# Query, key and value loads in one instruction, the output bias on TensorE

## The reference, cut to what matters

```python
def _L1_attn_ref(x, Wqkv, bqkv, Wout, bout):            # the second attention
    qkv = x @ Wqkv.T + bqkv
    ...                                                   # split into q, k, v of 16 heads
    attn = softmax(einsum('hbqd,hbkd->hbqk', q, k) * scale)
    o = einsum('hbqk,hbkd->hbqd', attn, v)
    return o_joined @ Wout.T + bout

def _L2_attn_ref(x, W_attn, W_proj):                      # the third attention
    q, k, v = split(x @ W_attn, 3)
    att = polymax(masked(einsum('bhid,bhjd->bhij', q, k) / sqrt(8)))
    # polymax(s) = (s*s + 1 if s > 0 else 1 - s/100) / 1000
    return einsum('bhij,bhjd->bhid', att, v) @ W_proj
```

## Time and profile before

| | |
|---|---|
| time, median of three runs | 1426.34 us |
| the profiled execution's own time | 1429.44 us |
| its span | 1427.6 us |
| TensorE busy in the span | 1166.2 us (82%) |
| VectorE busy | 1044.9 us (73%) |
| ScalarE busy | 727.0 us (51%) |
| GpSimd busy | 423.7 us (30%) |
| mean granted TensorE clock | 0.922 |
| second attention, about | 410 to 632 us of the span |
| third attention, about | 686 to 912 us of the span |

### The profile page before, as it was taken

One profiled execution on the slowest core, in us unless ns is written; L12 is line 12 of the kernel. 1 busy time (PEld: TensorE's weight loads), 2 busy tenths in 40 slices (PEclk: granted clock), 3 DMA queues, 4 the chain that ended last, 5 costly groups with the idle time before them and its releaser, 6 DMA issues.

```text
span 1427.6 us, 27186 instructions
## 1 busy us (share of the span) xinstructions
PE 1166.2 (82%) x9362; PEld 835.4 (59%) x9362; DVE 1044.9 (73%) x2899; ACT 727.0 (51%) x1186; POOL 423.7 (30%) x639
## 2 busy tenths in 40 slices
PE   5989898999987777758677878687779888888887
PEld 3666667888863333337444444576667445557776
DVE  7888875666666777736778998778886676768886
ACT  4445433333334666646476777443434566654442
POOL 5545441000033342212545554213122233201110
PEclk9999998999995999978798999798899899999999
DMA  8000000000000000000000000000000000000001
GB/s 344 1 1 1 1 1 0 0 0 0 0 1 1 1 1 0 1 1 1 1 1 1 0 1 2 1 1 1 1 1 2 1 3 0 2 2 1 1 1 30
DMA packets 5846, 14.64 MB, mean 10 GB/s; under 512 B 240, under 2 KB 4464, under 8 KB 5360
## 3 DMA queue, kind: packets, MB, share of 16 engines
q1 hardware_dynamic: 5744, 13.33, 2.5%
HBM read 12.28 MB, written 1.05 MB: 9 GB/s over the span
## 4 chain that ended last, share of the span: by engine, by line
issue 33%; PE 30%; DVE 18%; DVEq 6%; POOLq 5%; ACT 5%; POOL 4%; ACTq 0%
PE PS L1899 5%; PE PS L1908 3%; PE PS L1290 2%; PE PS L1203 2%; PE PS L1118 2%; POOL trs L416 2%; PE PS L1095 2%; PE PS L1487 1%; DVE w_l0f L2421 1%; PE PS L1224 1%; PE PS L1117 1%; PE PS L1230 1%; DVE sbuf L2089 1%; DVE h L1961 1%; DVE mx L2182 1%
## 5 line engine op out<-in xcount | busy, mean ns | idle before, releaser
L2182 DVE TENSOR_REDUCE mx<-PS 128x2 f32<-128x512 f32 (+1 forms) x256 | 155.1, 620 | 73.7 <-PE PS L1234 32.9
L737 ACT ACTIVATE w_l0f<-PS 128x512 f32<-128x512 f32 (+1 forms) x256 | 136.8, 543 | 96.1 <-PE PS L1241 46.7
L414 POOL TENSOR_TENSOR tve<-tmv,eps 128x2 f32<-128x2 f32 x64 | 14.7, 229 | 496.4 <-DVE tmv L1970 297.2
L1899 PE MATMUL PS<-hT_padded,w_l0f 128*128 128x256 f32 x512 | 122.2, 385 | 0.0
L1899 PEld LDWEIGHTS PS<-hT_padded,w_l0f 128*128 128x128 f32 x512 | 94.7, 194 | 11.0
L1027 ACT ACTIVATE sg<-PS 128x512 f32<-128x512 f32 x64 | 38.2, 597 | 120.3 <-PE PS L1899 120.3
L1658 PE MATMUL PS<-w_l2f,y 128*128 128x128 f32 x512 | 75.8, 295 | 18.7 <-ACT y L900 9.5
L1658 PEld LDWEIGHTS PS<-w_l2f,y 128*128 128x128 f32 x512 | 71.3, 208 | 26.7 <-ACT y L900 16.3
L2421 DVE SCALAR_TENSOR_TENSOR w_l0f<-w_l0f 128x768 f32<-128x768 f32 x64 | 67.5, 1055 | 17.8 <-ACT w_l0f L812 16.5
L3083 DVE TENSOR_TENSOR y<-sg,PS 128x512 f32<-128x512 f32 x64 | 43.9, 687 | 49.9 <-ACT sg L1027 42.6
L1908 PE MATMUL PS<-w_l0f,y 128*128 128x128 f32 x512 | 69.0, 278 | 6.1 <-DVE y L3083 6.1
(11 more groups left out here) (499 smaller groups left out, 3309.5 us busy)
## 6 DMA issues: line engine op xcount, KB each, us to landing
w_l0f<-in_l0f SPq DMA_DIRECT2D x1, 3076.0 KB, 17.7
w_l2f<-in_l2f SPq DMA_DIRECT2D x1, 2214.0 KB, 18.8
w_l3f<-in_l3f SPq DMA_DIRECT2D x1, 1736.0 KB, 22.6
w_l0a<-in_l0a SPq DMA_DIRECT2D x1, 960.0 KB, 7.6
result<-X SPq DMA_DIRECT2D x1, 896.0 KB, 4.6
X<-in_x SPq DMA_DIRECT2D x1, 768.0 KB, 10.9
PT<-in_cbf SPq DMA_DIRECT2D x1, 640.0 KB, 8.7
w_l1f<-in_l1f SPq DMA_DIRECT2D x1, 582.0 KB, 14.8
```

Of the source, the lines that this page charges most:

```text
L737: act.activation(P8[:, hh % 8, 0:width], PS[:, hh % 2, 0:width], ACT.Exp, scale=SM_SCALE).then_inc(a["pt"], 1)
L1899: ins = pe.matmul(PS[:, 2 * (c % 2) + g, b * L:(b + 1) * L], w("l0f", "w1")[:, at:at + P], hT[:], start=True, stop=True)
L2182: dve.tensor_reduce(mx[:, hh, 0:nm], PS[:, 2 + hh % 2, 0:nm * keys].rearrange("p (t k) -> p t k", t=nm), AX.X, ALU.max).then_inc(a["mx"], 1)
```

## The change

Queries, keys and values of a tile get one buffer with three parts, and there are two such buffers, which tiles use in turn. The first is new in name only (qf, kf and vf in one piece); the second lies in the last 768 columns of H1, a buffer that these layers don't use until the end of the third attention. With that, a load is one instruction of 3 x 128 columns. In the second attention the output bias is put into Y by a matmul of one row (a row of ones as weights, the bias as the moving row) ahead of the output projection, which accumulates on it; the statistics and the normalisation read Y in PSUM. In the third attention the factor 1/1000 moves from the load of the values to the copy of the outputs. The conditions that a load waits for are the same.

```diff
-        qf, kf, vf = (sb("qf", [P, T * NH, HD]), sb("kf", [P, T * NH, HD]), sb("vf", [P, T * NH, HD]))
+        qkv0 = sb("qkv0", [P, 3, T * NH, HD])
+        qf, kf, vf = (qkv0[:, n] for n in range(3))
...
-        vfs = (vf[:], cb_flat[:, 4 * 384:4 * 384 + T * NH * HD].rearrange("p (n d) -> p n d", d=HD))
+        qkvs = (qkv0[:], H1[:].rearrange("p n d -> p (n d)")[:, NB * T * D - 3 * T * D:]
+                .rearrange("p (k n d) -> p k n d", k=3, d=HD))
+        vfs = tuple(b[:, 2] for b in qkvs)
...
                         for t in range(T):
-                            ins = pe.matmul(Y[:, t, :], oT[:, t * P:(t + 1) * P], w(name, "wout"), start=True, stop=True)
+                            if l == L1_ATTN:
+                                pe.matmul(Y[:, t, :], w("const", "ones")[0:1, :], w(name, "bout")[0:1, :],
+                                          start=True, stop=False)
+                            ins = pe.matmul(Y[:, t, :], oT[:, t * P:(t + 1) * P], w(name, "wout"),
+                                            start=l == L3_ATTN, stop=True)
                         ins.then_inc(y_ready, 1)
...
                     def load_qkv(u, t, par, bank=7):
                         dve.wait_ge(a["qkv"], u * LOADS[l] + (t + 1))
+                        if l == L1_ATTN:
+                            three = lambda b: b.rearrange("p (k f) -> p k f", k=3)
+                            dve.tensor_tensor(qkvs[par][:, :, t * NH:(t + 1) * NH, :].rearrange("p k n d -> p k (n d)"),
+                                              three(PS[:, bank, 0:3 * D]), three(w(name, "bqkv")), ALU.add).then_inc(a["ld"], 1)
+                            return
...
                         dve.wait_ge(y_ready, u + (res0[l] + 1))
-                        if l == L1_ATTN:
-                            dve.tensor_tensor(acc[:], Y, w(name, "bout").unsqueeze(1).to_broadcast([P, T, D]), ALU.add)
-                            dve.drain()
-                        tail_stats(result)
+                        tail_stats(Y)
...
-                        dve.tensor_copy(qf[:, at], PS[:, bank, 0:D].rearrange("p (a d) -> p a d", d=HD))
-                        dve.tensor_copy(kf[:, at], PS[:, bank, D:2 * D].rearrange("p (a d) -> p a d", d=HD))
-                        dve.tensor_scalar(vfs[par][:, at], PS[:, bank, 2 * D:3 * D].rearrange("p (a d) -> p a d", d=HD),
-                                          1e-3, None, ALU.mult).then_inc(a["ld"], 1)
+                        dve.tensor_copy(qkvs[par][:, :, t * NH:(t + 1) * NH, :].rearrange("p k n d -> p k (n d)"),
+                                        PS[:, bank, 0:3 * D].rearrange("p (k f) -> p k f", k=3)).then_inc(a["ld"], 1)
...
                         for t in range(T):
-                            ins = dve.tensor_copy(ov[:, t], O[:, t, :, :, 0:HD])
+                            ins = dve.tensor_scalar(ov[:, t], O[:, t, :, :, 0:HD], 1e-3, None, ALU.mult)
```

More of the change, by code:

```diff
@@ L311, in within, with split_keys @@
             return not isinstance(i, int) or 0 <= i + u_off < NB
-        def split_keys(engine, l):
-            nk = KEY_HEADS[l]
+        def split_keys(engine, l, par=0):
+            nk, kf = KEY_HEADS[l], qkvs[par][:, 1]
             kn = slice(0, T * NH, NH) if nk == 1 else slice(0, T * NH)
@@ L329, in split_keys, with split_queries @@
             engine.sem_inc(AT[l]["ks"], 1)
-        def split_queries(engine, l, par):
+        def split_queries(engine, l, par, of=0):
+            qf = qkvs[of][:, 0]
             dst = QSs[par].rearrange("p n (s d) -> p n s d", d=HD)
@@ L2165, in load_qkv @@
                         dve.wait_ge(a["qkv"], u * LOADS[l] + (t + 1))
-                        at = 0
-                        for dst, width in ((qf[:], D), (kf[:], nk * HD), (vfs[par], nk * HD)):
-                            flat = dst.rearrange("p n d -> p (n d)")
-                            if l == L1_ATTN:
[L2170 to L2175, removed]
+                        if l == L1_ATTN:
[3 more added lines that the diff above has]
+                            return
+                        at = 0
+                        for dst, width in ((qf, D), (kf, nk * HD), (vfs[par], nk * HD)):
+                            ins = dve.tensor_copy(
+                                dst.rearrange("p n d -> p (n d)")[:, 0:T * width].rearrange("p (t f) -> p t f", t=T),
+                                PS[:, 7, 0:T * (D + 2 * HD)].rearrange("p (t f) -> p t f", t=T)[:, :, at:at + width])
                             at += width
@@ L3005, in load_behind @@
                         for t, bank in ((0, 4), (1, 7)):
-                            at = slice(t * NH, (t + 1) * NH)
-                            part = lambda n: PS[:, bank, n * D:(n + 1) * D].rearrange("p (a d) -> p a d", d=HD)
-                            dve.tensor_copy(qf[:, at], part(0))
-                            dve.tensor_copy(kf[:, at], part(1))
-                            dve.tensor_scalar(vf[:, at], part(2), 1e-3, None, ALU.mult).then_inc(behind["ld"], 1)
+                            dve.tensor_copy(qkv0[:, :, t * NH:(t + 1) * NH, :].rearrange("p k n d -> p k (n d)"),
+                                            PS[:, bank, 0:3 * D].rearrange("p (k f) -> p k f", k=3)).then_inc(behind["ld"], 1)
                     state_stats(1)
@@ L3095, in load_behind @@
                             dve.wait_ge(AT[L1_ATTN]["qkv"], t + 1)
-                            for n, dst in enumerate((qf, kf, vf)):
-                                flat = dst[:].rearrange("p n d -> p (n d)")
-                                ins = dve.tensor_tensor(flat[:, t * D:(t + 1) * D], PS[:, 6 + t, n * D:(n + 1) * D],
-                                                        w("l1a", "bqkv")[:, n * D:(n + 1) * D], ALU.add)
+                            three = lambda b: b.rearrange("p (k f) -> p k f", k=3)
+                            ins = dve.tensor_tensor(qkv0[:, :, t * NH:(t + 1) * NH, :].rearrange("p k n d -> p k (n d)"),
+                                                    three(PS[:, 6 + t, 0:3 * D]), three(w("l1a", "bqkv")), ALU.add)
                             ins.then_inc(AT[L1_ATTN]["ld"], 1)
```

14 lines of the change are left out of this document (6 added, 8 removed).

## The result

| | before | after |
|---|---|---|
| median of the runs | 1426.24 us (1420.34 to 1432.48, 9 runs) | 1433.67 us (1428.25 to 1435.37, 9 runs) |
| ratio after to before | | 1.0046, 95% interval 1.0029 to 1.0064 |
| span of the profiled execution | 1427.6 us | 1433.4 us |
| TensorE busy | 1166.2 us | 1181.0 us |
| VectorE busy | 1044.9 us | 1041.7 us |

The change made the kernel 7.4 us slower; 1423.0 was forecast, with 1432 as the upper end. Within 0.5% of before would have been up to 1433.5, so the result lies at that border, but the interval leaves no doubt of the sign.

The account below looks back on a forecast made before the run. No engine is full in the second attention, so the chain of waits binds; the third leans on VectorE. Loads (-1.8, -0.9, -0.5) and bias (-0.1) sum to -3.3 us, from 1426.34 to 1423.0; overall range 1413 to 1432.

Parts of the forecast that it names:

- Loads, 0.13 each: Merged query, key and value loads, second and third attention: each gives back 0.13 us, 3.2 us together.
- The rival that they pay 0.30 each: Loads on the path save each instruction's full recorded time, 0.30 us each, -7.5 in all: 1418.8 us; chance 0.08.
- Bias passes, 0.58: Second attention's output projection: four more TensorE passes a tile at 0.145 each cost 0.58 us, bounds 0 and 1.10.
- the slower rival: Bias passes cost more than 0.58 a tile; kernel slower from 0.99, 1427.2 us at 1.10; chance 0.15.
- The slack of 0.68: Second attention: queries' transposes could start 0.68 us earlier before the keys' copy limits them; 0.10 remains after the bias passes.
- VectorE's 0.48 not won: Second attention: dropping VectorE's bias addition frees 0.48 us, but a unit wins only 0.10 because the keys' copy holds it.
- The sum: Whole kernel: loads and bias terms add to -3.3 us, from the median 1426.34 to 1423.0 us.
- The clock rival: Second attention: shorter TensorE idle avoids six half-clock stretches, 1.3 us each, -7.8 in all: 1415.2 us; chance 0.25.
- The idle 1.21 before 530.13: Second attention: TensorE's 1.21 us wait for VectorE, ahead of a half-clock stretch, would shrink to about 0.15.
- Some for clock stretches that come instead of going: Part of the 0.13 chance of a slower kernel: new half-clock stretches appear; no size given.
- Hidden anyway: Loads' gain is lost to the next wait, such as GpSimd's chain or a later clock fall: 1426 us; chance 0.07.
- What would show it: Signs: load near 0.555 us, project-out group near 1.29; wrong if half-clock stretches aren't six or a pass exceeds 0.25.

Follow-up runs that it names:

- after_va: Changed kernel plus unread extra matmuls in the second attention and, in the third, GpSimd copying values before splitting the next keys; 1419.12 us, ratio 0.9941 to before.
- before_va: Kernel before plus unread extra matmuls in the second attention and, in the third, GpSimd copying values before splitting the next keys; 1418.72 us, ratio 0.9933 to before.
- after_fill_end: Changed kernel plus 24 unread extra matmuls in one unit, the last with maxima in the second attention; 1427.27 us, ratio 0.9996 to the kernel before.
- loads_only: Changed kernel with the second attention's output bias given back to VectorE, merged loads kept; 1434.87 us, ratio 1.0058 to the kernel before.
- bias_only: Kernel before with only the output bias moved to TensorE, loads, buffers and scaling as before; 1431.61 us, ratio 1.0027 to the kernel before.
- the copy's order alone: Kernel before with only GpSimd's copy of the values put ahead of the key split in the third attention; 1428.22 us, ratio 0.9994 to before.

## Why the prediction was wrong, step by step

Two steps failed. The bias passes were put at 0.58 us a tile and took 1.03, and the sum left TensorE's clock where it had been in one trace of the kernel before. With the first put right the change is worth about nothing; the larger part of the 7.4 us is the second.

- **Loads, 0.13 each.** Right, to the hundredth: 0.557 recorded, 0.47 to the successor, 1.3 us for ten loads in five units at full clock. The rival that they pay 0.30 each fell with that: five units would have gained 3.0. Its size came from recorded durations, and these overlap. The starts give another: 128 columns more take (0.47 - 0.20)/2 = 0.135 us, so of the 0.20 from one start to the next some 0.065 are fixed (an estimate from these rows), and two of them are the 0.13. The rule of the Trainium skill ("VectorE: DVE Perf Modes", section on the TRN2 errata), that a fixed latency is exposed between instructions, is written there for operations that read SBUF; these read PSUM and agree with it in kind, with a part of 0.065.
- **Bias passes, 0.58.** This term failed in size. I took 0.145 a pass from a neighbour in which passes of one shape follow each other; one-row passes between full ones cost 1.03 for four (0.26 each), and in the last tile, at half clock, 1.74 for the 0.85 forecast. The right value was within the bounds (1.10) and above the break-even of the slower rival: its own formula gives 8 x 1.03 - 7.9 = +0.3 us, some 1426.7. The slack of 0.68 that I allowed was real in the unit shown: beside the group's +1.03, the queries' transposes stand only 529.25 - 524.30 = 4.95 behind its start, where they stood 530.46 - 525.72 = 4.74.
- **VectorE's 0.48 not won.** Right in place: the keys' copy is what they wait for now. With 128 rows the whole bias is worth 0.0 in five units, for a forecast of -0.5.
- **The sum.** This is the step that decided. Priced anew from rows, the change comes to +2.1 us, an estimate: loads -3.2 as forecast (of which 1.3 are shown), five units +2.8, the sixth +0.1 by its formula, the seventh +1.0, the last +1.4. The pair after_va and before_va says +0.4. Measured were +7.4, so some 5 to 7 us are none of its terms. The sum treated the clock as given, in the units and outside them. That the clock holds the rest is shown from one side: 24 matmuls in the waits of one unit take some 7 us away. In the trace the 17.1 us at half clock from 599.6 and the lower clock up to 705.7 belong to it; the 27.3 us at half clock in the fourth attention can't be laid to the change.
- **The clock rival** had its price right and its condition wrong. Five units take their length at full clock and 1.1 to 1.5 us more for each stretch at half clock in them: the kernel before 111.5 with none and 118.7 with five, the changed kernel 113.0, 116.4 (after_fill_end, ahead of its extra matmuls) and 119.5 with none, three and five, that with the 128-row bias 110.2 and 112.6 with none and two. I had 1.3. The idle 1.21 before 530.13 did shrink, to the 0.34 before 529.25, and in this trace the falls stayed; in those of loads_only and bias_only most of them went. There are seven stretches from 460.7 to 600.7 in the kernel before, not the six that I counted. My sentence that the trace agrees, as far as two stretches show, with a fall after standing idle rested on little: TensorE was busy 1.69 of the 3.40 us ahead of the fall, so it had not stood idle throughout. I gave a chance to the clock's getting better and next to none to its getting worse, though the profile of before had stretches at half clock at the end of each stage. "Some for clock stretches that come instead of going" was the outcome, at a few per cent.
- **Hidden anyway** named "the clock falling later" at 0.07. It named the clock, but bounded it wrongly: I let it take the gain and no more, while loads_only loses more than the gain (1.0058, with less work on VectorE and nothing added).
- **What would show it.** The project-out group (1.67 for 1.29) and the pass over 0.25 were named as marks of a wrong forecast and both came. The second attention's half-clock stretches were to be six: six of 3.4 us are there, and then the one of 17.1, where the kernel before has its seventh of 3.4.

Left open: how the change keeps the clock down at the end of the second attention, and why loads_only, which adds nothing to TensorE, is as slow as the changed kernel. Its trace lays that to the third attention's four long units, and these go with the key split's 2.68 us; what brings the split beside VectorE's long instructions I haven't isolated. Nor did I try the 24 matmuls, or the copy's order alone, on loads_only.

## What to carry to other kernels

Where the granted clock of a software-pipelined stage falls once in a unit, price an edit by the units' length at full clock and the falls apart (1.1 to 1.5 us each here), and give the clock a chance in both directions, at the ends of stages above all. Test it with matmuls that do nothing in TensorE's waits: they separate what an edit costs from what it sets off, and may be worth more than the edit (some 7 us in the changed kernel, 9 in the kernel before); elsewhere they can cost as much. One trace of a kernel doesn't show how many falls it meets as a rule. A matmul's duration holds only among neighbours of its shape: a one-row pass between full ones cost over twice one of 128 rows.

## What the hardware showed that I had not expected

- A bias by one row takes longer than one by 128 rows: 1.67 against 1.09 us for the group of eight passes, and the kernel some 8.7 us longer.
- Half-clock stretches can return every 23.9 us (second attention) or 27.3 us (third) for a whole stage, and be absent from some of the same units in another execution of the same code (after_fill_end, ahead of its extra matmuls): units of the second attention, all traces taken together, last 23.2 to 24.5 us with one of 3.4 us in them and 21.7 to 22.9 without.
- TensorE at 1.2 GHz was busy 14.62 of 17.10 us, and its clock did not come back in that stretch.
- The first instruction of GpSimd's key split took 2.68 us where two of VectorE's 768-column instructions ran beside it, and 0.94 where none did, while those kept their 0.95. Later in such a unit of before_filled one of VectorE's took 1.57.
